# Pool's zero-fill copies described as four times 128 rows of 2.5 KB

## The reference, cut to what matters

```python
x = layernorm(x + L0(x, edge_index, edge_weight, W0, b0))           # weighted sum over edges
x = layernorm(x + L1(x, edge_index, edge_type, basis, att, ...))    # two layers, gated, 2 relations x 30 bases
x = layernorm(x + L2(x, edge_index, W, b))                          # degree-normalised sum over edges
x = layernorm(x + L3(x, edge_index, edge_attr_8, Wq, ..., bo))      # attention along edges, 8 heads
```

## Time and profile before

| | |
|---|---|
| median of 3 runs | 1247.96 us (1245.73 to 1251.37) |
| the profiled execution, its own time | 1259.67 us |
| its span, first to last instruction | 1257.9 us |
| mean granted TensorE clock | 0.982 |
| TensorE busy | 1181.3 us, 94% |
| Pool busy | 307.6 us, 24% |
| queue 0 (Pool): packets, MB, share of 16 engines' span | 25184, 53.10, 16.7% |
| queue 1 (SP) | 34706, 156.38, 35.8% |
| queue 10 (ScalarE) | 4350, 12.07, 2.8% |

### The profile page before, as it was taken

The page is one execution under the profiler, slowest core; times in us unless marked ns, Lnnn a source line. Parts: engine busy times, 40 slices in busy tenths (PEclk is TensorE's granted clock), DMA queues, the critical chain, the costliest instruction groups (busy, mean ns, idle before and its releaser), DMA issues.

```text
span 1257.9 us, 21464 instructions
## 1 busy us (share of the span) xinstructions
PE 1181.3 (94%) x8083; PEld 540.5 (43%) x8084; DVE 851.3 (68%) x1330; ACT 437.1 (35%) x586; POOL 307.6 (24%) x220
## 2 busy tenths in 40 slices
PE   6987879999999999999999999999999899999997
PEld 2333334323344334345445454455333365555553
DVE  7575657544434555553368875575999889899997
ACT  2444546512122222112311002216553255444454
POOL 2000000000010133344655655545556000000000
PEclk9988989999999999999999999999999899999999
DMA  8567867598799789753122213112223376565653
GB/s 327 209 217 247 297 224 269 151 407 305 243 363 307 257 285 314 278 165 109 2 35 35 50 19 69 2 3 33 34 33 67 139 235 231 202 220 187 213 186 112
DMA packets 64325, 222.73 MB, mean 177 GB/s; under 512 B 31138, under 2 KB 36002, under 8 KB 48272
## 3 DMA queue, kind: packets, MB, share of 16 engines
q1 hardware_dynamic: 34706, 156.38, 35.8%
q0 software_dynamic: 25184, 53.10, 16.7%
q10 hardware_dynamic: 4350, 12.07, 2.8%
HBM read 198.92 MB, written 59.92 MB: 206 GB/s over the span
## 4 chain that ended last, share of the span: by engine, by line
PE 69%; DVE 11%; issue 7%; DMA 7%; ACT 3%; SPq 2%; DVEq 1%; ACTq 0%
PE PS L1853 26%; PE PS L1802 10%; PE PS L1727 6%; PE PS L1657 5%; PE PS L2098 4%; PE PS L2085 4%; DMA R<-R 4%; DVE R L1172 4%; DVE R L1209 4%; PE PS L1675 3%; PE PS L1967 2%; PE PS L2144 2%; PE PS L1889 1%; PE PS L1773 1%; DMA W<-in_basis_s 1%
## 5 line engine op out<-in xcount | busy, mean ns | idle before, releaser
L812 POOL DMA_INDIRECT bias_d<-R x160 | 271.0, 1694 | 331.3 <-DMA bias_d<-R 220.5
L1853 PE MATMUL PS<-R 128*128 128x512 f16 x1300 | 298.1, 381 | 0.0
L1853 PEld LDWEIGHTS PS<-R 128*128 128x128 f16 x1300 | 120.5, 98 | 180.6 <-issue 49.7
L1727 PE MATMUL PS<-R,XX 125*128 125x512 f16 (+2 forms) x612 | 134.7, 354 | 15.3 <-ACT R L1400 6.8
L1613 ACT ACTIVATE R<-PS 128x1024 f32<-128x1024 f32 (+1 forms) x100 | 106.2, 1087 | 109.6 <-PE PS L2085 77.9
L1802 PE MATMUL PS<-W,XX 128*128 128x512 f16 x600 | 136.0, 386 | 5.1 <-DVE R L1010 2.7
L926 DVE TENSOR_SCALAR R<-W,R 125x1250 f16<-125x1250 f16 x160 | 89.4, 606 | 53.7 <-PE PS L1727 39.4
L1172 DVE CUSTOM_DVE_ANT_0 R<-PS,R 128x1250 f16<-128x1250 f32 x80 | 116.8, 1459 | 5.5 <-PE PS L2021 2.9
L2098 PE MATMUL PS<-R 128*32 128x256 f32 (+1 forms) x1600 | 102.5, 391 | 5.2 <-DVE R L1209 5.2
L2085 PE MATMUL PS<-R 128*128 128x256 f16 (+3 forms) x800 | 99.6, 275 | 5.4 <-ACT R L1613 2.2
L779 POOL DMA_DIRECT2D bias_d<-bias_d x39 | 21.6, 556 | 324.0 <-PE PS L1727 164.2
(11 more groups left out here) (231 smaller groups left out, 1411.0 us busy)
## 6 DMA issues: line engine op xcount, KB each, us to landing
bias_d<-bias_d POOLq DMA_DIRECT2D x39, 1280.0 KB, 9.0
R<-in_basis_s SPq DMA_DIRECT2D x32, 1024.0 KB, 6.9
W<-in_basis_s SPq DMA_DIRECT2D x28, 1024.0 KB, 6.1
W<-bias_d SPq DMA_DIRECT2D x27, 1024.0 KB, 4.9
XX<-bias_d SPq DMA_DIRECT2D x13, 1024.0 KB, 4.9
R<-key_d SPq DMA_DIRECT2D x20, 500.0 KB, 4.0
R<-R SPq DMA_DIRECT2D x120, 80.0 KB, 5.9
W<-bias_d SPq DMA_DIRECT2D x7, 904.0 KB, 4.6
```

The costliest lines, as they stand in the source:

```text
L812: pool.indirect_dma_start(bias_d, bass.IndirectOffsetOnAxis(ap=idx[:, c:c + 1], axis=0), attr[:, c, :], None, bounds_check=DUMP + GC * P - ...
L1727: ins = T.matmul(mm_out(3 * (j % 2) + b, p1 - p0), own[0:EC, bass.ds(c, 1), :, :].rearrange("p c m w -> p (c m w)"), hots(p0, p1), start=f ...
L1853: ins = T.matmul(mm_out(SUM_BANK(s, i), D), lhs, rhs, start=n == 0, stop=n == len(terms) - 1)
```

## The change

The cells, the number of copies, their order and their waits stay. Only the form of each of the 39 copies from cell 0 differs. Before, source and destination are each 128 rows of 2560 numbers, one behind the other without a gap. After, each is 4 x 128 rows of 640 numbers: the outermost dimension (b) steps by 2.5 KB, the middle one (p) by 10 KB, so that a row does not join the next.

```diff
--- before.py
+++ after.py
@@ -776,7 +776,8 @@
                                    zero.rearrange("p (u n) -> p u n", u=1).broadcast_to([P, 2, NN])).then_inc(
                                        zero_out, 16)
                 else:
-                    pool.dma_start(cells[n], cells[0]).then_inc(zero_out, 16)
+                    pool.dma_start(cells[n].rearrange("p (b e) -> b p e", e=NN // 2),
+                                   cells[0].rearrange("p (b e) -> b p e", e=NN // 2)).then_inc(zero_out, 16)
 
 
             for i in range(2):
```

## The result

| | before | after |
|---|---|---|
| median, fastest and slowest of 5 runs | 1249.17 us (1245.73 to 1251.37) | 1255.99 us (1255.06 to 1257.68) |
| ratio of the runs | 1 | 1.0058, 95% interval 1.0038 to 1.0077 |
| the profiled execution, its span | 1259.67, 1257.9 us | 1255.99, 1254.3 us |

The change makes the kernel slower, by 0.6%, where a gain of 1.4% was forecast. The two profiled executions say the opposite of the runs: the span fell by 3.6 us.

A forecast was written before the change was run, and what follows sets the result against it. Late R<-R copies behind Pool's 40 KB fill packets were taken to hold up the loop; -19.4 there and +1.5 at the weights gave -18 us, so 1230 us at the median, range 1219 to 1249.

The forecast's parts named there:

- What bounds the loop: Loop over 40 tiles: late R<-R copies out of stage16, slowed by Pool's zero fill, cost 19.4 us.
- The term of the loop, -19.4: Loop over 40 tiles: small packets leave no stage16 slot late, saving 19.4 us, bounds 0 and -19.4.
- Nine turns: Loop: engines alternate queues by packet; a tile's R<-R waits nine turns, 17 us before, 1.1 after, landing in about 3.
- How many engines: Zero copies: outermost dimension 4 probably puts each on four engines, 15 us (13 to 22) in place of 9.
- cost in the loop: 0, covered by the spacing: Loop: slower zero copies on successive fours keep up, 24 copies in 150 us, so they cost nothing.
- cost 0 for the last eleven: Copies issued together at 355.87: 54 us in place of 51, with 78 us free before the scatter; cost 0.
- Weights, +1.5: Load W<-w_d beside zero copies on four engines: 12 us in place of 10.96, +1.5, bounds -1.7 and +9.
- Pool's own time: Pool's issue of each zero copy takes 1.4 us, upper bound 6.2; free at 1.4.
- D: Rival, 7%: all 39 copies queue on the same four engines, the scatter waits for the fill, 1419 us.
- E: Rival, 3%: Pool's issue takes 6.2 us per copy, so L800, needed by VectorE, is 8.5 us late; 1239 us.
- B: Rival, 12%: packet size is only part; the fill keeps half the engines' time, R<-R stays late half as much; 1239 us.

The follow-up runs named there:

- before again: The kernel before, unedited, run and profiled a second time: median 1250.70 us, ratio 1.0009 to the kernel before.
- the changed kernel again: The changed kernel, unedited, run and profiled a second time: 1258.19 us, ratio 1.0051 to the kernel before.

## Why the prediction was wrong

**What bounds the loop: right.** The late R<-R copies were what the loop lost. Without 40 KB packets L1399 did not wait for them (but for one wait of 1.3 us in the ten profiles, with 20 KB and two copies moved), and 39 intervals took 153 to 154 us. In the changed kernel no interval was slow but four extra visits, and TensorE was granted 1.00 of its clock (2.4 GHz) from 75 to 229 us, where the kernel before had 0.91 from 75 to 115 and from 155 to 195.

**The term of the loop, -19.4: mis-sized.** It measured 10.4 us, so it was 9.0 too large. It was read from one execution, and that was 10 us above the median of its own runs. I noted the difference and carried all 19.4 over to the median; 163.4 and 163.8 us in the two later profiles of that packet length, against 170.3, show that some 7 us of this excess were in this very term. The other 2 are extra visits: I counted two intervals, and four of 4.9 us stay in the changed kernel, so that the loop took 153.0 us and not 151.

**Nine turns: not shown, in part wrong.** R<-R did not land in 3 us: the medians are 6.0, 5.7 in the changed kernel, 5.4 with 20 KB. What the packet's length changes is seen on SP's queue. SP's issues in the profile of before again (start, us of issuing, copies):

```profile
127.23 3.04 SPq L627 DMA_DIRECT2D R<-R  x1
130.32 1.40 SPq L629 DMA_DIRECT2D R<-R  x2
131.76 3.90 SPq L627 DMA_DIRECT2D R<-R  x1
135.70 2.63 SPq L629 DMA_DIRECT2D R<-R  x2
```

and in the changed kernel:

```profile
193.53 0.51 SPq L627 DMA_DIRECT2D R<-R  x1
194.08 1.22 SPq L629 DMA_DIRECT2D R<-R  x2
197.32 0.51 SPq L627 DMA_DIRECT2D R<-R  x1
```

Added up over the loop's 120 copies, SP's issuing takes some 139 us in the profile of before again, against a loop of 163; it takes 84 with 20 KB packets, 89 in the changed kernel and 72 with 5 KB on 16 engines. So SP is at times held 3 to 4 us in one issue and falls behind the tiles (3.81 us each). Why an issue is held that long was not isolated. The nine turns are not refuted either: with 20 KB rows a packet held an engine 0.95 us, nine are 8.5 us and the slot is wanted after 15.2, so turns too would give no loss at 20 KB and one at 40 KB.

**How many engines: right, and its price not.** The stores' eight completions pointed to four engines, and that successive copies take different fours is borne out: queue 0 kept 53.3% of 16 engines' time, more than one four could give. 20.1 us to landing lie within the 13 to 22 given. But "cost in the loop: 0, covered by the spacing" is the step that failed, and cost 0 for the last eleven rests on the same assumption: that Pool can issue whenever its turn comes. It is held after seven copies, until all of them have landed. What this puts off, five copies at 202 us, runs into the loop's end. The last R<-R, issued at 228.96, landed at 239.46. The share of busy engines (tenths, 40 slices of 229 to 241 us) is 9 until 237, with the late fill and SP's own loads, and then drops to 2, as much as four of 16:

```profile
DMA  7999999899998999999999999975442222222299
```

R<-R and the basis load together are 9.6 us which stood nowhere in my sum. With the last five on 16 engines both were as short as before (8.4 us less than in the changed kernel again), and the whole kernel was 7.6 us faster.

**Weights, +1.5: wrong, the bound was the value.** I gave 9 us as the worst case, with all of a copy's packets still to go, and took 1.5 from the copy issued 8 us before. It was the second copy, issued at 332.87, 1 us after the load began, that had everything to go. 64 packets of 0.20 us in turn with the load's 5 us are 18 us; 19.10 was measured, 18.11 with nothing but these two copies changed. That the two copies cause the long load is shown by that kernel. That they do it by turns is not, because SP was held too. Its four issues of L636, in before again and in the changed kernel:

```profile
331.52 2.04 SPq L636 DMA_DIRECT2D W<-w_d  x4
```

```profile
330.08 9.40 SPq L636 DMA_DIRECT2D W<-w_d  x4
```

The chain's W<-w_d is the last of these four loads, counted from the start of its issue. That issue alone took 7.87 us in the changed kernel, and 6.8 to 8.9 in every kernel with both late copies on four engines; it took 0.51 in all others. The third load, whose issue was not held, landed after 11.6 us where it was 9.7. Whether the turns or the held issue set the 19 us was not isolated.

**Pool's own time: right.** 1.4 us forecast, 1.1 to 1.2 measured.

**The rivals.** D needed all copies on one four. It came in another way: holds move the fill's end, and in two experiments the scatter did wait for it. In the changed kernel itself it did not. Nor did E come there: Pool had made the ramp by 398.0, and VectorE's first key comparison ran at 412.78. B is refuted: the fill still held half of the engines' time, 53.3%, and the waits for R<-R were gone. Spread over 16 engines the same rows took 1239.09 us, over four 1255.99, a difference of 17. The Trainium skill's rule ("DMA: Bandwidth & Descriptors", Rules for kernel authors), to put a dimension of a multiple of 16 outermost, agrees with that.

**Sum, by its own steps.** Forecast -19.4 + 1.5 = -18. Measured, profile against profile: -10.4 + 9.6 + 7.9 - 1.4 = +5.7. In the runs +6.8.

## What to carry to other kernels

A long background copy should be cut into packets short enough that the urgent queue is not held (here 20 KB did, 40 KB did not), and yet lie over all 16 engines with few rows for each: length and spread are two settings, and the outermost dimension decides the second. Two copies on four engines, issued beside a load that the critical path waits for, can cost as much as all 39 short packets gain. Before a term is carried from a profile to the median, a second profile of the same kernel tells whether the term is the kernel's or that execution's.

## What was not expected of the hardware

- A copy with 4 outermost came with 768 packets of 8 bytes, three for each of its 256 full ones (with 10 KB rows, 14,976 packets of 4 bytes over 39 copies beside 4,992 full ones). That they went to the twelve engines without data fits the counts; the trace does not name the engine.
- Rows of 2.5 KB went two to a packet; rows of 5, 10, 20 and 40 KB one to a packet.
- Pool stood for 12 to 40 us between copies once some 900 to 960 rows for an engine had been given out: after each 7th copy with 128 rows for an engine, after the 30th with 32. It went on 0.4 to 0.7 us after all copies given out had landed; of the 30, 28 had landed long before.
- With two copies on four engines beside it, SP took 6.8 to 8.9 us to issue the last of four loads of 512 KB, against 0.51 us otherwise.
- The loop's loss has a step and no slope in the packet's length: 153 us at 5, 10 and 20 KB, 163 to 170 at 40 KB.
